# Gathered rows turned by transposing transfers on SyncE instead of by TensorE and ScalarE

## What is computed

```python
xn = _layernorm(x, axis=-1)
x = x + _L0_attn_ref(xn, ...) + _L0_ffn_ref(xn, ...)
...
logits = jnp.einsum('th,eh->te', x, gate_w)
scores = jax.nn.softmax(logits, axis=-1)
topk_w, topk_idx = jax.lax.top_k(scores, K)
...
g = jnp.einsum('th,ehi->tei', x, w_gate)
u = jnp.einsum('th,ehi->tei', x, w_up)
a = jax.nn.silu(g) * u
a = a * combine[:, :, None]
y = jnp.einsum('tei,eih->th', a, w_down)
...
y = y + jax.nn.silu(sg) * su @ sw_down
```

## Time and profile before

| what | value |
|---|---|
| median of three runs | 1182.44 us |
| profiled execution: span of its records (the page gives no other time for it) | 1354.9 us |
| TensorE busy | 1007.9 us, 74% of the span |
| VectorE busy | 866.0 us, 64% |
| ScalarE busy | 654.5 us, 48% |
| GpSimd busy | 579.2 us, 43% |
| mean granted TensorE clock | 0.880 |

### The profile page before, as it was taken

The page is one execution under the profiler, slowest core; times in us unless marked ns, Lnnn a source line. Parts: engine busy times, 40 slices in busy tenths (PEclk is TensorE's granted clock), DMA queues, the critical chain, the costliest instruction groups (busy, mean ns, idle before and its releaser), DMA issues.

```text
span 1354.9 us, 26394 instructions
## 1 busy us (share of the span) xinstructions
PE 1007.9 (74%) x8634; PEld 525.7 (39%) x8634; DVE 866.0 (64%) x1784; ACT 654.5 (48%) x1219; POOL 579.2 (43%) x531
## 2 busy tenths in 40 slices
PE   2788121010399999898998989998988989899885
PEld 1555010000144444444544444454444445444433
DVE  6888831000288887777777676676767676677553
ACT  3778100000154545565566666556666665566341
POOL 6333177776200000454366666435656553464100
PEclk9888555555599999899999999999989999899888
DMA  6899450010113131443545355354535353444702
GB/s 175 270 297 283 125 180 1 1 34 1 43 56 105 54 104 48 88 85 75 89 80 112 63 111 95 66 89 78 111 57 112 56 112 64 88 71 73 134 17 31
DMA packets 99484, 126.41 MB, mean 93 GB/s; under 512 B 24873, under 2 KB 83514, under 8 KB 98834
## 3 DMA queue, kind: packets, MB, share of 16 engines
q0 software_dynamic: 41632, 60.79, 25.0%
q1 hardware_dynamic: 57730, 63.99, 16.1%
HBM read 71.63 MB, written 57.80 MB: 96 GB/s over the span
## 4 chain that ended last, share of the span: by engine, by line
PE 53%; DVE 10%; another core or an unknown queue 10%; issue 9%; ACT 2%; SPq 1%; DMA 1%; POOL 0%; ACTq 0%; DVEq 0%
PE gup L1221 12%; PE pvp L1144 10%; PE outs L1248 9%; DVE part L1314 6%; PE smp L1100 6%; PE turn L1233 4%; PE stp L1125 4%; PE outs L1151 3%; PE turn L1191 3%; PE smp L1083 1%; ACT probs L1484 1%; DVE hf L1371 1%; DVE sg L1366 1%; DMA Qs<-nm 1%
## 5 line engine op out<-in xcount | busy, mean ns | idle before, releaser
L1484 ACT ACTIVATE probs<-stp 128x1024 f32<-128x1024 f32 (+1 forms) x320 | 300.4, 939 | 424.4 <-remote 205.2
L1314 DVE TENSOR_REDUCE part<-smp 128x2 f32<-128x256 f32 (+2 forms) x372 | 345.9, 951 | 140.0 <-remote 72.5
L942 POOL DMA_INDIRECT XG<-xrow_d,slots x144 | 146.8, 1019 | 247.0 <-DMA out<-Y 201.7
L1221 PE MATMUL gup<-gu_w,XC 128*128 (+1 forms) x1152 | 212.8, 321 | 32.7 <-issue 21.8
L1100 PE MATMUL smp<-Ks,Qs 48*128 48x128 f16 (+2 forms) x744 | 112.5, 341 | 103.7 <-DVE part L1314 52.4
L1248 PE MATMUL outs<-dn_w,h 88*128 (+1 forms) x1248 | 183.6, 280 | 0.1
L949 POOL DMA_INDIRECT out<-Y,slots x72 | 117.1, 1626 | 139.1 <-ACT Y L1517 107.8
L1144 PE MATMUL pvp<-probs,Vs 128*32 128x512 f32 (+3 forms) x1536 | 168.8, 512 | 0.8 <-DVE probs L1413 0.7
L949 POOL DMA_INDIRECT acc_d<-Y,slots x72 | 114.7, 1594 | 123.7 <-ACT Y L1517 104.6
L1221 PEld LDWEIGHTS gup<-gu_w,XC 128*128 128x128 f16 x1152 | 107.2, 99 | 96.1 <-issue 43.5
L931 POOL DMA_INDIRECT slot_d<-entry,slot_i x128 | 124.3, 971 | 41.6 <-issue 41.6
(11 more groups left out here) (170 smaller groups left out, 1109.6 us busy)
## 6 DMA issues: line engine op xcount, KB each, us to landing
rb<-rsum_d SPq DMA_DIRECT2D x60, 128.0 KB
Ks<-k_d SPq DMA_DIRECT2D x96, 64.0 KB
Qs<-q_d SPq DMA_DIRECT2D x96, 64.0 KB
v_d<-V SPq DMA_DIRECT2D x8, 544.0 KB, 4.6
Vs<-v_d SPq DMA_DIRECT2D x16, 272.0 KB, 3.0
acc_d<-YA SPq DMA_DIRECT2D x1, 4224.0 KB
X<-L_attn_x POOLq DMA_DIRECT2D x8, 512.0 KB, 5.0
xrow_d<-XR SPq DMA_DIRECT2D x8, 512.0 KB, 5.0
```

What stands on the lines that cost most here:

```text
L942: pool.indirect_dma_start(XG[:, q].rearrange("p a c t -> p (a c t)"), None, s.xrow_d, bass.IndirectOffsetOnAxis(ap=slots[:, r, 0:1], axis= ...
L1221: last = pe.matmul(gup[:, 0:2 * I], columns[:, a, h], weights_of(s.gu_w, e, b, h, slice(0, 2 * I)), start=n == 0, stop=n == 5)
L1314: last = dve.tensor_reduce(part[:, g % 2, k0 // CH, :, j, t], banks[:, :, col:col + w], AX.X, ALU.max)
L1484: act.activation(to, of, ACT.Exp, scale=float(DK) ** -0.5 / QS ** 2).then_inc(exp_done, 1)
```

## The change

The rows of a routed tile are still gathered by GpSimd, now into six buffers instead of eight. SyncE then turns a gathered tile with one transposing transfer from XG to XC. XC is a ring of four buffers through which all 176 tiles go in order, shared and routed; each is loaded or turned three units ahead of the first unit that uses it (LEAD), after the last unit of the tile four places before it has done its gate and up, and after its gather has landed. TensorE's turning of rows, ScalarE's copies and the waits that went with them are gone. The planner's cost of a routed first half becomes that of a shared one, and the first ten gathers are issued in one loop ahead of GpSimd's waits, each from the seventh on after the transposing transfer of the tile six before it has landed.

```diff
-        GB, AHEAD = 8, 10
+        GB, AHEAD = 6, 10
         XG = sb("XG", [P, GB, 2, HC, P], F16)
-        XC = sb("XC", [P, 2, 2, HC, P], F16)
+        CB, LEAD = 4, 3
+        XC = sb("XC", [P, CB, 2, HC, P], F16)
...
-        xp = turn[:, 0:2 * P].bitcast(F16)
...
+        def tile_of(v):
+
+            u = shared_of(v)
+            return ST + v - SU if u is None else u // SH if u < SU else UT + u // SH
+
+        FIRST_UNIT = [next(v for v in range(NV) if tile_of(v) == x) for x in range(ST + UT + KT)]
+        LAST_UNIT = [FIRST_UNIT[x] + (1 if ST <= x < ST + UT else SH) - 1 for x in range(ST + UT + KT)]
+
+        def tiles_loaded_at(v):
+
+            return [x for x in range(ST + UT + KT) if FIRST_UNIT[x] - LEAD == v]
+
+        def columns_in(x):
+            return xc_in[x % CB], 16 * (x // CB + 1)
...
-            cost = [(880 if shared_of(v) is not None else 1200, 980)[h] for h, v in halves]
+            cost = [(880, 980)[h] for h, v in halves]
...
             def gather(r):
                 q = r % GB
                 if r >= GB:
-                    pool.wait_ge(xp_done, r - GB + 1)
+                    pool.wait_ge(*columns_in(ST + r - GB))
...
-            for r in range(GB):
+            for r in range(AHEAD):
                 gather(r)
...
             for r in range(UT):
-                if r == 0:
-                    for x in range(GB, AHEAD):
-                        gather(x)
                 scatter_add(r)
...
+            def columns(x):
+                if x >= CB:
+                    sp.wait_ge(gu_done, LAST_UNIT[x - CB] + 1)
+                to, done = XC[:, x % CB], columns_in(x)[0]
+                if ST <= x < ST + UT:
+                    r = x - ST
+                    sp.wait_ge(xg_in[r % GB], 16 * (r // GB + 1))
+                    sp.dma_start_transpose(to.rearrange("p a c t -> p (a c) t"),
+                                           XG[:, r % GB].rearrange("p a c t -> p (a c t)")).then_inc(done, 16)
+                else:
+                    sp.dma_start(to.rearrange("p a c t -> p (a c t)"), s.xcol_d[x if x < ST else x - UT]).then_inc(done, 16)
...
             def after_first(v):
-                if v < SU and v % SH == SH - 1 and v // SH + 2 < ST:
-                    shared_columns(v // SH + 2)
-                r = v + 1 - SU
-                if UT - GB <= r < UT:
-                    late_columns(ST + r - (UT - GB))
+                for x in tiles_loaded_at(v):
+                    columns(x)
...
-            def turn_rows(r):
-                q = r % GB
-                pe.wait_ge(xg_in[q], 16 * (r // GB + 1))
-                pe.wait_ge(hl_done, turned_h[0])
-                if turned_rows[0]:
-                    pe.wait_ge(xc_done, turned_rows[0])
-                for a in range(2):
-                    for h in range(HC):
-                        o = (a * HC + h) * P
-                        last = pe.transpose(xp[:, o:o + P], XG[:, q, a, h], s.ident16[:, :])
-                last.then_inc(xp_done, 1)
-                turned_rows[0] += 1
...
+                x = tile_of(v)
+                if v == FIRST_UNIT[x]:
+                    pe.wait_ge(*columns_in(x))
+                columns = XC[:, x % CB]
...
-            def columns(r):
-                act.wait_ge(xp_done, r + 1)
-                act.wait_ge(gu_done, SU + r - 1)
-                act.activation(XC[:, r % 2].rearrange("p a c t -> p (a c t)"), xp, ACT.Copy).then_inc(xc_done, 1)
```

More of the change, by code:

```diff
@@ L910, in attention_and_experts @@
         xg_in = [sem(f"xg_in{i}") for i in range(GB)]
-        xc_in = [sem("xc_in0"), sem("xc_in1")]; xs_in = [sem("xs_in0"), sem("xs_in1")]
+        xc_in = [sem(f"xc_in{i}") for i in range(CB)]; xs_in = [sem("xs_in0"), sem("xs_in1")]
         sel_made = sem("sel_made"); floored = sem("floored"); inverted = sem("inverted"); spread = sem("spread")
-        late_in = [sem(f"late_in{i}") for i in range(GB)]
-        xp_done = sem("xp_done"); xc_done = sem("xc_done"); gu_done = sem("gu_done"); th_done = sem("th_done")
+        gu_done = sem("gu_done"); th_done = sem("th_done")
         sg_done = sem("sg_done"); hf_done = sem("hf_done"); hT_done = sem("hT_done"); hh_done = sem("hh_done"); hl_done = sem("hl_done")
@@ L1047, in _ @@
             sp.dma_start(s.out[ST * P:T, :], s.xf[ST * P:T, :]).then_inc(cleared, 16)
+            for x in range(ST):
+                if FIRST_UNIT[x] < LEAD:
+                    columns(x)
             for t in range(2):
-                shared_columns(t)
                 shared_rows(t)
@@ L1179, in _ @@
             experts = {}
-            turned_rows, turned_h = [0], [0]
-            def turn_rows(r):
-                q = r % GB
-                pe.wait_ge(xg_in[q], 16 * (r // GB + 1))
-                pe.wait_ge(hl_done, turned_h[0])
-                if turned_rows[0]:
-                    pe.wait_ge(xc_done, turned_rows[0])
-                for a in range(2):
-                    for h in range(HC):
-                        o = (a * HC + h) * P
-                        last = pe.transpose(xp[:, o:o + P], XG[:, q, a, h], s.ident16[:, :])
-                last.then_inc(xp_done, 1)
-                turned_rows[0] += 1
             def load_expert(r):
@@ L1234, in turn_h @@
                 last.then_inc(hT_done, 1)
-                turned_h[0] += 1
             def down(v, projected):
@@ L1283, in _ @@
                     if a is not None:
-                        if SU <= a + 1 < SU + UT:
-                            turn_rows(a + 1 - SU)
                         gate_up(a)
@@ L1525, in _ @@
                     if a is not None:
-                        if SU <= a + 1 < SU + UT:
-                            columns(a + 1 - SU)
                         gates(a)
```

## The result

The changed kernel takes 1194.3 us (median of 19 runs, 1187.6 to 1207.5) against 1182.5 us of the kernel before on the same chips: a ratio of 1.0092, 95% interval 1.0069 to 1.0115. It is slower by some 11 us. The forecast was 1152, faster. The result lies inside the range of 1110 to 1300, but on the other side of no change than was forecast. Of the rivals, SyncE as the bound is out: it waits 213.5 us for TensorE's gate and up matmuls. The time is at the upper edge of the band of 1165 to 1195 that the late reciprocals were given, but not by that rival's sum, in which they eat a gain of 55 us; there was no such gain.

A forecast was written before the change was run, and what follows sets the result against it. The prediction took TensorE, 91% busy in the routed stretch, as the bound. Its terms, -55 for the turning, +20 for late reciprocals and +5 for the maxima, gave -30 us: 1182.4 to about 1152, range 1110 to 1300.

The forecast's parts named there:

- the late reciprocals: Rival: on SyncE's queue, reciprocals delayed by turned tiles eat the whole gain of 55 us, about 1182; chance 0.15.
- What the change removes: TensorE in the routed stretch: 576 transposes, 57.8 us, and 15.1 us idle before them go; gain 55 us.
- ScalarE's copies and the waits: ScalarE: 144 copies, 85.3 us, run beside gate and up matmuls; TensorE waited 2.9 us for them; counted at nothing.
- t = 1.7 us: SyncE's time to issue one transposing transfer, taken near four ordinary transfers in sequence; bounds 0.35 to 11.3 us.
- rival one: SyncE's queue of transposes, or the transfer itself, becomes the bound from t = 3.6 us; slower, about 1305 or 1520; chance 0.35.
- Step (1): Turned tiles for gate and up come just in time, 18.5 us needed of 18.7 available; costs nothing.
- Step (2): Reciprocals behind three tiles on SyncE's queue go out 1.7 us late a period, delaying VectorE; 20 us lost.
- Step (3): The next period's maxima can find SyncE in the middle of an issue, and the scores wait; 5 us lost.
- Step (4): SyncE waits for a tile's gather, holding up its queue; mean margin 10.5 us suffices, GpSimd's buffer wait costs nothing.
- Step (5): DMA engines carry 18.9 MB more beside the 64 MB of SyncE's queue, 5% more; not a limit.
- The planner's cost: Cost of a routed first half, 1200 becoming 880, shifts units by a few slots and adds no work; nothing.
- the forecast case: Tiles turned on SyncE's queue with TensorE's gain mostly kept: about 1152 us, own range 1110 to 1172; chance 0.50.

The follow-up runs named there:

- b_one_of_four: The kernel before with one transpose of a routed tile instead of four, waits and ScalarE's copy kept: 1178.8 us, ratio 0.9987.
- b_no_turn: The kernel before without any turning, neither transposes nor copy, matmuls reading the gathered rows as they are: 1155.8 us, ratio 0.978.
- b_one_no_copy: The kernel before with one transpose of a routed tile, the shared bank's wait kept, and no copy on ScalarE: 1173.8 us, ratio 0.9946.
- b_no_copy2: The kernel before with the four transposes and their wait for the shared bank kept, ScalarE's copy left out: 1174.9 us, ratio 0.9937.
- b_again: The kernel before, unchanged, run for a second profile: 1177.0 us, with a profiled span of 1175.4.

## Why the prediction was wrong

**What the change removes: the step that failed.** I took 55 us between 38 and 73, because "nothing covers them, since the engine is 91% busy". Leaving all the turning out wins 26 (22 to 30 by the interval), below the lower end. Two things were wrong. The price: 576 times 224 ns is 129 us, not 57.8, and that mismatch in one row says that its durations overlap. The 57.8 us are the time in which at least one of the transposes was running, 144 runs of 0.40 us; the next matmuls start after 0.23 us, so TensorE was held for 33 us. The chain's 2.8%, my lower bound, was taken from the same durations. And the cover, which weighs as much: a busy share of 91% is not a bound. With three quarters of the transposes gone TensorE's busy time fell by 14.4 us and its idle time rose by 14.2 (b_one_of_four); with all the turning gone its waits for VectorE's reductions grew by 18 (b_no_turn).

**ScalarE's copies and the waits, counted at nothing.** The copy with TensorE's waits for it is worth 7 us, and some 20 us hang on the first transpose with its wait for the shared bank. That last share is a remainder of b_no_turn over b_one_no_copy; the profile of b_no_copy2 shows 15 us of waiting for VectorE, and what of the 20 it makes up is not told apart. I had added the 15.1 us of idle time in front of the turn to the upper end alone and not asked what ended it.

**t = 1.7 us.** It measured 1.21 (median of 144). The right kind of row was chosen, and rival one, for which t had to be 3.6, falls. The Trainium skill, "VectorE: DVE Perf Modes" (The three transpose paths), has 1309 ns for a block of 128x128; a whole tile of four was issued in 1.2 us here and TensorE waited for tiles 2.3 us in all, so four blocks don't cost four times that one after the other.

**Step (1), the tiles in time: right.** With 2.3 us of waits in all.

**Step (2), late reciprocals: the mechanism right, the number by luck.** I forecast 20 us, and moving the loads gives back 21. But the 20 stood on t = 1.7 (three of which are 5.1 us, not 5.2; a matter of 1 us in the 20). With the measured 1.21 my own formula has 3 x 1.21 = 3.6 us against a slack of 3.5, next to nothing. VectorE started with rb 1.6 us later a period all the same, since the store and the rb loads landed more slowly too. What I also left out is what follows a stall: TensorE idles behind VectorE, and its matmuls after it run at half the clock (1.94 us for six instead of 1.07), which makes up about half of what the move gives back.

**Step (3), the maxima: small, as said.** TensorE waited 10.0 us for them against 7.7. **Step (4), the gathers: right.** SyncE waited for them 8.7 us over nine times. GpSimd's wait for a free buffer, which I had at nothing, is 32.5 us in three waits ahead of its first scatter; it then stands another 11.4 us for the first result that it can scatter, so they cost nothing. **Step (5), the DMA engines: a size wrong, of little weight.** I had 5% more from SyncE's queue; its packets went from 57,730 to 136,066 and their share from 18.2% in b_again to 28.0%, since a turned tile moves as 512 packets of 256 bytes. Undoing that is worth some 4 us once the queue is in order, which the intervals don't tell from nothing. **The planner's cost, counted at nothing,** loses some 3 us.

**Sum.** In place of -55 + 20 + 5: -26 for the turning, +21 for the place of the loads with the clock, +4 for the packets, +3 for the planner. That makes +2 where +11 was measured. The 9 us between them stay open. They are not much more than the intervals of these differences leave together. Two candidates were not tested: the smaller ring of gather buffers, and the move of the loads, which cost 8 us in the kernel before and, if it costs as much in this one, hides that much of the loss in SyncE's queue. The stated range of the forecast case was also too narrow by its own terms: with t = 2.2 and a gain of 38 the three terms are -38 + 37 + 7, so 1188 and not 1172. The closest rival was "the gain is eaten by late reciprocals". It named the place and gave 1182, because it took the gain for 55.

## What to carry to other kernels

The duration of a matmul or transpose in a row is not what it costs in a run: subtract a run of n from a run of 2n, or look at the time from the start of one run to the start of what follows. Even that is only what the engine is freed of. Here 91% busy was not yet the bound, and freed time turned into waiting, so ask what the engine will wait for next before any of it is called a gain; the sure test is a kernel that leaves the work out. Look also at what the first of a run waits for, even where the profile says "issue". Work that is moved to a queue with time to spare still has a place in that queue's program order: ask what stands behind the new items at the moment when the queue has no pause, and move what isn't urgent (here loads that are needed a whole period later) behind what is. A stall of a busy TensorE can be paid twice: here one of 4.4 us was followed by some 2 us at half the clock.

## What the runs showed of the hardware

A transposing transfer of a 128x512 fp16 tile within SBUF was issued in 1.21 us by SyncE (median of 144, 1.19 to 2.58), against 0.35 us for the plain load of a tile, and moved as 256-byte packets of 21.8 ns on average. At 638 to 646 us, with transposing transfers and rb under way, the DMA share of the stretch reached 1.19.

One transpose of 128x128 fp16 on TensorE alone took 0.23 us, four in a run 0.40 and eight 0.62. The Trainium skill, "TensorE: Matmul & The Clock Gate" (Wait — 56ns, not 53.3ns?), has 56 ns from one 128-column matmul to the next; the 0.055 us here agree. By that figure 576 transposes are an estimated 32 us and not 57.8, which would have mended the price in the first term of the sum, though not the cover.

Around the end of a stand of 4.43 us TensorE's granted clock fell to 0.50, where it was from 645 to 647 us, and the six gate and up matmuls took 1.94 us instead of 1.07. The Trainium skill, "TensorE: Matmul & The Clock Gate" (What's actually happening), has 2.4 GHz for a busy and 1.2 GHz for an idle TensorE; the rows agree with both levels.
